# Splitting weights between gathers: the low parts of root, Wout and the gate's first part on GpSimd instead of VectorE

## The reference, cut to what matters

```python
# L1 gnn, xn = layernorm(x): 10625 edges of 8 types
out = xn @ root + bias
for r in range(8):
    mask = (edge_type == r)
    sums = segment_sum(xn[src] * mask, dst); cnt = segment_sum(mask, dst)
    out = out + (sums / max(cnt, 1)) @ weight[r]
u = out
z = concat([u, xn]) @ w_gate + b_gate
h = tanh(u) * z + xn * (1 - z)
# L1 mix: linear attention over 16 heads, then
mix = heads @ Wout + bout
x = x + h + mix
```

## Time and profile before

| | |
|---|---|
| median of 3 runs | 2518.72 us (2518.45 to 2530.13) |
| the profiled execution's own time | 2521.97 us |
| its span, first to last instruction | 2520.1 us |
| TensorE matmul busy | 2438.6 us, 97% |
| VectorE busy | 1811.3 us, 72% |
| ScalarE busy | 1421.7 us, 56% |
| GpSimd busy | 653.3 us, 26% |
| mean granted TensorE clock | 0.989 |

### The profile page before, as it was taken

The page is one execution under the profiler, slowest core; times in us unless marked ns, Lnnn a source line. Parts: engine busy times, 40 slices in busy tenths (PEclk is TensorE's granted clock), DMA queues, the critical chain, the costliest instruction groups (busy, mean ns, idle before and its releaser), DMA issues.

```text
span 2520.1 us, 32144 instructions
## 1 busy us (share of the span) xinstructions
PE 2438.6 (97%) x12692; PEld 2019.6 (80%) x12692; DVE 1811.3 (72%) x2006; ACT 1421.7 (56%) x1890; POOL 653.3 (26%) x538
## 2 busy tenths in 40 slices
PE   7999998999999999999998999999999979999999
PEld 6978788777777777777787777777899977777797
DVE  7449664888878888788868876556567778887453
ACT  5327432777677767777733344443377758884131
POOL 5758204434431000000021005442000016556000
PEclk9999999999999999999999999999999999999999
DMA  6334026999999899999974344445211138884212
GB/s 176 78 100 129 1 80 216 332 337 334 350 352 350 336 335 336 360 390 374 354 216 158 104 155 137 118 135 162 91 44 56 54 114 277 285 275 142 92 56 74
DMA packets 128013, 508.14 MB, mean 202 GB/s; under 512 B 26892, under 2 KB 44697, under 8 KB 101240
## 3 DMA queue, kind: packets, MB, share of 16 engines
q1 hardware_dynamic: 78440, 418.00, 46.2%
q0 software_dynamic: 34928, 74.92, 10.5%
q10 hardware_dynamic: 14496, 13.17, 1.6%
HBM read 458.93 MB, written 46.88 MB: 201 GB/s over the span
## 4 chain that ended last, share of the span: by engine, by line
PE 84%; DVE 8%; DMA 3%; issue 2%; ACT 2%; POOL 1%; SPq 0%; DVEq 0%; ACTq 0%
PE ps L231 83%; DVE od L262 2%; DMA scr_ei<-xn,sdi 1%; DVE Aw L258 1%; DVE x L258 1%; DMA wk<-in_Wk 1%; DVE ua L258 1%; PE ps L2025 1%; PE ps L1236 1%; DMA gr<-scr_y,gidx 1%; POOL scr_ei L2228 1%; DVE zq_l L270 0%; PE ps L1993 0%; DVE ws_l L270 0%; ACT gh L2308 0%
## 5 line engine op out<-in xcount | busy, mean ns | idle before, releaser
L270 DVE TENSOR_TENSOR pr_l<-pr,hs 128x1408 fp32r<-128x1408 f32 (+1 forms) x455 | 645.5, 1444 | 137.3 <-ACT hs L793 134.5
L793 ACT ACTIVATE hs<-pr 128x1408 fp32r<-128x1408 f32 (+1 forms) x455 | 559.0, 1242 | 205.3 <-PE ps L231 164.5
L793 ACT ACTIVATE ws_h<-wr 128x1024 fp32r<-128x1024 f32 (+1 forms) x105 | 110.2, 1051 | 206.7 <-PE ps L231 199.6
L270 DVE TENSOR_TENSOR ws_l<-wr,ws_h 128x1024 fp32r<-128x1024 f32 (+1 forms) x103 | 129.8, 1261 | 115.4 <-ACT ws_h L793 115.2
L231 PE MATMUL ps<-hs,xe_h 128*98 128x512 f32 (+1 forms) x768 | 205.5, 376 | 0.0
L231 PE MATMUL ps<-pr_l,xe_h 128*98 128x512 f32 (+1 forms) x768 | 205.0, 375 | 0.0
L231 PE MATMUL ps<-hs,xe_l 128*98 128x512 f32 (+1 forms) x768 | 204.6, 374 | 0.0
L2234 POOL DMA_DIRECT2D xin<-scr_ei x16 | 9.4, 590 | 581.1 <-PE ps L1993 550.3
L231 PEld LDWEIGHTS ps<-pr_l,xe_h 128*98 128x98 f32 x768 | 124.8, 163 | 38.8 <-DVE pr_l L270 0.9
L231 PEld LDWEIGHTS ps<-hs,xe_l 128*98 128x98 f32 x768 | 125.0, 163 | 38.2
L231 PEld LDWEIGHTS ps<-hs,xe_h 128*98 128x98 f32 x768 | 123.8, 163 | 36.7
(11 more groups left out here) (476 smaller groups left out, 6263.6 us busy)
## 6 DMA issues: line engine op xcount, KB each, us to landing
pr<-in_wg SPq DMA_DIRECT2D x64, 1408.0 KB, 7.9
pr<-in_wu SPq DMA_DIRECT2D x64, 1408.0 KB, 8.4
pr<-in_wd SPq DMA_DIRECT2D x80, 1024.0 KB, 6.8
B<-in_rel SPq DMA_DIRECT2D x64, 512.0 KB, 3.4
scr_y<-y SPq DMA_DIRECT2D x45, 448.0 KB
pr<-in_wd_last SPq DMA_DIRECT2D x16, 512.0 KB, 5.2
wr<-in_Wqkv SPq DMA_DIRECT2D x16, 512.0 KB, 5.4
wr<-in_gate SPq DMA_DIRECT2D x16, 512.0 KB, 3.4
```

The lines of the kernel that those rows point to most:

```text
L270: return e.tensor_tensor(lo, src, hi.bitcast(F32), ALU.subtract)
L793: q.e.activation(c.hi, c.at, ACT.Copy).then_inc(*self.s("high").up(c.key))
```

## The change

Eighteen of the twenty chunks of the window, all but root's first two, are marked for GpSimd: chunks 2 to 19. VectorE leaves their low parts out; GpSimd makes them in `p_rows` with the same subtraction, between the gathers. The low part of chunk `b` is put ahead of the first gather `c` (from 6 on) whose awaited sum `c - 6` lies in slot `10 b - 13` or later. What is left of the list after the last gather follows there, ahead of the loads of `xnk`. The later parts of the gate stay with VectorE.

```diff
         for n in ("root", "Wout"):
             for h in range(2):
                 for i in range(4):
-                    W.add((n, h, i), a[n][h, i], 1024, 3)
+                    W.add((n, h, i), a[n][h, i], 1024, 3, pool=(n, h) != ("root", 0) or i > 1)
...
                     if (h, part, i) == (1, 0, 3):
                         W.add(("zgate", h, part, i), a["gate"][part, h, i], 1024, 3, keep=(m["zgp_h"], m["zgp_l"]))
                     else:
-                        W.add(("zgate", h, part, i), a["gate"][part, h, i], 1024, 3)
+                        W.add(("zgate", h, part, i), a["gate"][part, h, i], 1024, 3, pool=(h, part) == (0, 1))
...
         q.wait_ge(self.s("attention_sums"), ("out", 7, 0))
+        lows = [(key, slot) for b, key, slot in self.blocks() if b > 1]
         for c in range(NW):
+            while lows and c >= NR and SUM0 + (c - NR) * (SUM1 - SUM0) // NW >= lows[0][1] - 13:
+                self.p_low(q, lows.pop(0)[0])
             if c >= NR:
                 q.wait_ge(self.s("summed"), (c - NR, 1))
             elif c > 1:
                 q.wait_ge(self.s("out_low"), 7)
             of = bass.IndirectOffsetOnAxis(ap=m["gidx"][:, c:c + 1].bitcast(U32), axis=0)
             e.indirect_dma_start(m[f"gr{c % NR}"], None, self.d_y[:, :], of).then_inc(*self.landed(f"rows{c % NR}").up(c))
+        for key, slot in lows:
+            self.p_low(q, key)
```

## The result

The changed kernel takes **2582.98 us** (median of 4 runs, 2579.54 to 2584.12), the kernel before in the same comparison 2518.59 us (median of 4, 2514.01 to 2530.13). The ratio is 1.0258 with a 95% interval of 1.0235 to 1.0282: 64.4 us slower. Predicted were 2590 us, range 2564 to 2614. The profiled execution has a span of 2581.0 us, 60.9 more than the one before, and a mean clock of 0.982.

What follows compares the result with a forecast made beforehand. TensorE was taken as the bound, with 4.3 to 7.4 us idle in the window. Terms 56.5 + 9 - 2 + 7.5 = +71 us on the 2518.72 us median gave 2590 us, range 2564 to 2614.

Steps and rivals of the forecast that it cites:

- The ring: Window: low part, gathers, fourth `gh`, next high part form a loop; 16.7 or 18.5 us per period against 13.05, +56.5 us.
- ScalarE's pace: In the ring: 1.77 us per group, three groups 5.3 us where gathers take 4.8; used in the period's lower bound, 15.5.
- The start: Window's start: chunk 2's low part goes ahead of gather 6, so chunk 4's high part ends late, +9 us.
- The last sums: After chunk 18's high part: the last sums follow in about 6 us instead of 8, -2 us.
- The end: Window's end: `xnk` loads stand behind chunk 19's low part and come late for `ua - xnk`, +7.5 us.
- VectorE beside GpSimd: Window: SBUF contention slows VectorE's operations (3.45 against 1.23 us), but VectorE is outside the ring; costed at nothing.
- Rival 2: Window: contention alone, ring hidden, VectorE becomes the bound; 16 us plus 7.5 at the end, 2542 us; chance 0.08.
- Rival 1: Window: GpSimd's idle time holds the low parts; up to 7.4 us won, 7.5 lost behind, 2511 to 2520 us; chance 0.05.
- The clock: Window: TensorE's idle time each period may bring half speed, 1.7 us of work, still below the ring's period; nothing in sum.
- Rival 3: Window: TensorE's slow clock joins the ring, 1 to 1.5 us more a period, 2605 to 2612 us; chance 0.12.
- GpSimd's wait for `ws_h`: Sign in the window: GpSimd waits 3 to 4 us for ScalarE ahead of most of its 18 subtractions.

Runs made afterwards that it cites:

- e1: Changed kernel with low parts placed later in GpSimd's list (slot 10 b - 6 instead of 10 b - 13): 2536.32 us, +22.4 over the kernel before.
- e3: Changed kernel with VectorE making all low parts again; GpSimd only waits for the high part at the old places: 2550.45 us, +36.5 over the kernel before.
- e11: Changed kernel with 76 one-column GpSimd memsets after each wait for the high part instead of subtractions, VectorE making low parts: 2573.27 us, +57.8 over the kernel before.
- e2: As e1, with the ten loads of xnk also put ahead of the leftover low parts: 2534.38 us, +20.5 over the kernel before.
- e5: Changed kernel with only the ten loads of xnk put ahead of the leftover low parts: 2577.84 us, +62.8 over the kernel before.
- e4: Kernel before with nobody making low parts of chunks 2 to 19, readers waiting for high parts, output wrong: 2506.09 us, -7.8.
- e10: As e9, but each memset block replaced by a low-part-sized GpSimd subtraction on its own buffer: 2534.74 us, +19.3 over the kernel before.
- e9: Changed kernel, late places (- 6), no wait for high parts, 76 one-column GpSimd memsets per subtraction, VectorE making low parts: 2518.32 us, +2.9 over the kernel before.

## Why the prediction was right

The time, the sign and the mechanism held. The terms, measured in the two profiles:

| term | predicted | measured |
|---|---|---|
| 14 periods of the ring | +56.5 | 239.43 - 182.69 = +56.7 |
| start, high part of chunk 2 to that of chunk 4 | +9 | 33.48 - 26.71 = +6.8 |
| last sums, high part of chunk 18 to that of 19 | -2 | 11.88 - 11.88 = 0 |
| end, high part of chunk 19 to first matmul on `u` | +7.5 | 23.24 - 17.58 = +5.7 |
| sum | +71 | +69.2 |

These are differences of two single profiles. The stretch behind the first matmul on `u` is 210.0 us before, 211.0 with the change and 206.3 in e1, so terms of 2 or 3 us are at the edge of what they can tell.

- **The ring.** 16.7 and 18.5 us were forecast for four and five gathers; measured were 16.57 and 19.04. In the turn shown, the gathers were quicker than ScalarE: the landing of the first (5.61) and three groups of ScalarE (5.31) set it, not the issue of the fourth and its landing (4.8 + 6.5). The two ways give almost the same sum, 10.9 and 11.3, so the total held by luck although its inside was wrong: what I had named only as a lower bound, ScalarE's pace, is the path. The other turns show the same: in all fourteen ScalarE waits for the rows of the first gather behind the low part, in two of them also, for 0.3 and 0.7 us, for those of the second, and in none for the fourth. From that first `gh` to the next high part it takes 6.35 to 6.51 us in seven of the eleven turns with four gathers. What the other four have above this, and the three with five gathers above the 8.12 of the shortest, is 5.4 us together, of 56.7. e3 and e11 show the ring itself, e1 that it goes with the place of the low part.
- **The start** was oversized by 2.2 us. The high part of chunk 3 comes 16.77 us after that of chunk 2, and that of chunk 4 16.71 after that, which is a normal turn. The first low part took 2.39 us and not the 3.2 that I had put in, and it began 7.5 us after the high part of chunk 2, where I had 9.0.
- **The last sums.** No gain: TensorE's own work held the high part of chunk 19 as before.
- **The end** was oversized by 1.8 us: the loads landed 5.05 us after their issue, where the fastest of before took 6.9. The mechanism is shown by e2 and e5.
- **VectorE beside GpSimd** was costed at nothing inside the ring; e11 and the change differ by 0.3 us a period. But the prediction called this cost hidden and did not say how near it was. Rival 2, contention alone, had a price of 2542 us, +23; with the ring gone e1 measured +22.4. The price held by luck, the reason did not: VectorE is not full (169.98 us of 200 in e1); single long `gl` let TensorE wait.
- **Rival 1**, at most 7.4 us to win: e4 shows 7.8. But even without a ring the time doesn't stay, as e1 shows.
- **The clock** fell to 0.92, so stretches at 1.2 GHz lie among those at 2.4. TensorE was busy for 84% of the window, where I said 75 to 80%: 853 matmuls at 0.234 us are 199.6 us, 76%, and most of the other 21 us must be the low clock (the same count leaves 3.1 us of 200 before, at 1.00). I put its cost at nothing. No run tries that by itself; but e3's window has a clock of 0.99, and its ring costs 36.5 us all the same. The 5.4 us above bound what a late TensorE can have put between the first `gh` and the high part; 4.6 of them lie in turns with a clock of 0.82 to 0.91, but other turns with such a clock have none. Rival 3's extra 1 to 1.5 us in each period is not seen.
- **GpSimd's wait for `ws_h`** was given as 3 to 4 us; it is 6.0 in the mean (96.5 in 16), 4.2 in the turn shown. The issue of gathers took 1.16 us in the mean and not 1.31, and so GpSimd was sooner back at the wait.

The spans differ by less than 69.2, by 60.9. In the profile of before the first expert matmul starts at 437.0 us, after at 428.1: 9 us ahead of the window and of everything that the change touches, a difference between executions (in the thirteen profiles this point lies between 424.8 and 440.0). The medians differ by 64.4 us, between the two; 2590 was 7 us too high.

## What to carry to other kernels

Idle time of an engine that works a list in order is only free room for work whose inputs are there when its turn comes; before moving an instruction, write down what stands behind it and whether that leads back to its own input, since one such loop makes each turn at least as long as itself (here 17.10 us in place of 13.05; a mere wait alone makes it 15.32). Place such work as late as its reader allows, not as early as its buffer does. And price the neighbours too: an instruction that costs its new engine nothing may lengthen the ones beside it on another engine that feeds the bound.

## What the runs showed of the hardware

- A two-input subtraction on GpSimd of 128x1024 takes 2.41 us and stretches a two-input operation of VectorE that lies fully beside it from 1.28 to 3.61 us (e1), by about its own length: in the rows of e1, of e10 and of the change one of the two always waits for the other to end. VectorE spends less by making the 1.22 us subtraction itself.
- 76 memsets of one column on GpSimd take 2.2 us together, 0.03 us each (e9): not a way to make a delay in a few instructions.
- The issue of a gather takes 1.75 to 1.77 us right behind GpSimd's subtraction, 16 times of 16 in 2060 to 2360 of the changed kernel. Of the 78 other gathers there, 61 take 0.94 to 0.95, the rest up to 1.89.
- Two gathers issued 1.3 us apart landed 4.4 and 7.4 us after issue, with the load of a chunk starting between them (e3).
